# First transfers of the attention: the second stack and one chunk of parts go ahead of the first maxima, two chunks go behind them

## The chip, the cores and the metric

The kernel is one program on one core of a Trainium2 chip. The metric is the time of one execution on the device in microseconds (us), lower is better. The engines are TensorE (PE, with its weight loads PEld), VectorE (DVE), ScalarE (ACT), GpSimd (POOL) and SyncE (SP), which issues nearly all DMA transfers of this kernel.

## What is computed

`x` has 4 sequences of 1024 tokens, 128 wide. The first layer is a causal attention with 16 heads of 8 (the weights go through a rank of 32), between two layer norms and with a residual. The second is two layers of windowed attention and a gated MLP, again between layer norms. The change touches the first layer alone:

```python
x = x + _layernorm(_L0_attn_ref(_layernorm(x), W_dq, W_uq, W_dkv, W_uk, W_uv, W_o))
# in _L0_attn_ref
Q, K, V = (c_q @ W_uq), (c_kv @ W_uk), (c_kv @ W_uv)      # heads of 8
scores = einsum('bqhd,bkhd->bhqk', Q, K) / sqrt(8)         # causal, 1024 x 1024 per head
attn = softmax(scores); out = einsum('bhqk,bkhd->bqhd', attn, V) @ W_o
```

## The kernel before

`project` (L83 to L297) norms the tokens, projects them to Q, K and V, and cuts each f32 value of Q and K into three bf16 parts. It does so in 8 chunks of 512 tokens (two chunks are one sequence). `send_parts` (L72) writes the parts of one chunk to DRAM with six DMAs of 128 KB, three of q (L77) and three of k (L79). The SBUF buffer of parts has 4 places, so chunk 5 is in place 1.

`load_group` (L64) reads them back as a **stack** for one sequence and one group of four heads, with the nine products of parts laid out as 72 rows: one DMA of 576 KB for q (L69, with `q_src` as 24 x 3 x 4096) and one for k (L70, with `k_src` as 3 x 24 x 4096). A stack needs only the chunks of its own sequence, that is chunks 0 and 1 for the first four stacks.

`attend` (L363 to L634) works through 16 stages (4 sequences x 4 head groups) of 12 groups each. For each stage PE makes the scores twice: first `max_unit` (L431, 48 units a stage) into `a_psM`, which DVE reduces to a row maximum (L598, L600), and later `score` (L443) into `a_psE`, which ACT turns into exponentials (L515). The negated maxima reach the second pass as 12 more rows of the q stack. For that POOL cuts them in three, PE turns them (L469), ACT copies them to `a_nmT` (L521), and SP sends them with one DMA of 48 KB into rows 72 to 83 of `a_qs` (`send_maxima`, L398). A stage has two such halves, (s, 0) and (s, 1). `values` (L457) multiplies the exponentials with V two to three groups later.

PE does the first 32 `max_unit`s, turns the maxima (0, 0), and then begins group 0, whose first score waits for `nm_in[0]`, the landing of the maxima (0, 0). The first score of group 4 waits for the maxima (0, 1), that of group 12 for the maxima (1, 0). `max_unit` 48, the first of the second stage, is in group 2 and waits for the second stack.

All this is one hand-written order on SP, and one SP queue carries it. In `project` SP sends chunks 0 to 3, loads the first stack and sends chunk 4. In `attend` it sends chunks 5, 6 and 7, loads the second stack, and then

```python
def send_maxima(s, half):
    sp.wait_ge(e_read, nm_slot(s, half) + 1)      # ACT has copied a_nmT
    ...
    sp.dma_start(qs[ROWS:KROWS, s % NG, :, cols], nmT[...]...).then_inc(nm_in[half], 16)
```

sends the maxima (0, 0) and (0, 1), loads stacks 2 and 3, and waits for the parts of all places (`parts_out`) before the loop over the later stages.

Of the kernel before, what the change touches and what calls it, by code (L numbers as in the profile page):

```python
# [28 lines left out]
NCH = NT // 4  # L29
# [34 lines left out]
def load_group(sp, io, sb, b, g):  # L64

    into = sb["stack_in"][g]
    q_src = io["q_parts"][b, g].rearrange("a d j n -> (a d) (j n)").unsqueeze(1).broadcast_to((3 * DK, 3, HG * S))
    k_src = io["k_parts"][b, g].rearrange("d r j n -> (d r) (j n)").unsqueeze(0).broadcast_to((3, 3 * DK, HG * S))
    sp.dma_start(sb["qs"][0:ROWS, g, :, :], q_src).then_inc(into, 16)  # L69
    sp.dma_start(sb["ks"][0:ROWS, g, :, :], k_src).then_inc(into, 16)  # L70


def send_parts(sp, io, sb, c):

    pair, place, cols, parts_out = c // 2, c % PARTS, slice(512 * (c % 2), 512 * (c % 2) + 512), sb["parts_out"]
    for a in range(3):
        sp.dma_start(io["q_parts"][pair, :, a, :, :, cols].rearrange("g d j n -> g (d j) n"),  # L77
                     sb["parts"][:, place, 0, a, :]).then_inc(parts_out[place], 16)
        sp.dma_start(io["k_parts"][pair, :, :, a, :, cols].rearrange("g d j n -> (g d) j n"),  # L79
                     sb["parts"][:, place, 1, a, :]).then_inc(parts_out[place], 16)  # L80
# [255 lines left out]
def nm_slot(s, half):  # L336

    G = nm_turn_group(s, half)
    before = sum(1 for s2 in range(NSTAGE) for h2 in range(2) if nm_turn_group(s2, h2) < G)
    return (G + 1) * HG + before  # L340
# [19 lines left out]
def attend(nc, io, sb):  # L360


    with ExitStack() as ctx:  # L363
# [29 lines left out]
        @block.sync  # L393
        def _(sp):
            def send_maxima(s, half):
                sp.wait_ge(e_read, nm_slot(s, half) + 1)
                cols = slice(512 * half, 512 * half + 512)
                sp.dma_start(qs[ROWS:KROWS, s % NG, :, cols], nmT[:, s % 2, cols].unsqueeze(1).broadcast_to((NM, HG, 512))).then_inc(nm_in[half], 16)  # L398

            for c in range(5, NCH):  # L400
                send_parts(sp, io, sb, c)
            load_group(sp, io, sb, 0, 1)
            send_maxima(0, 0)
            send_maxima(0, 1)
            for g in range(2, NG):
                load_group(sp, io, sb, 0, g)
            for place in range(PARTS):
                sp.wait_ge(sb["parts_out"][place], 16 * 6 * (NCH // PARTS))
            for e in range(NSTAGE):
                if e + 1 < NSTAGE:  # L410
                    send_maxima(e + 1, 0)
                if e > 0 and e + NG - 1 < NSTAGE:
                    sp.wait_ge(av_done, e * NGR)
                    load_group(sp, io, sb, (e + NG - 1) // NG, (e + NG - 1) % NG)
                if e + 1 < NSTAGE:
                    send_maxima(e + 1, 1)
            for half in range(2):
                sp.wait_ge(nm_in[half], 16 * NSTAGE)
# [1138 lines left out]
```

## Time and profile before

| what | value |
|---|---|
| median of 3 runs | 1483.54 us (1483.34 to 1484.93) |
| the profiled execution, its own time | 1486.43 us |
| its span, first to last instruction | 1484.7 us |
| `project` up to the first matmul of the attention | 0 to 68.7 us |
| the attention's groups, first to last | 100.1 to about 580 us |
| granted TensorE clock, mean | 0.933 of full |

One execution was profiled; all durations below are from it. The span leaves out some 1.7 us around the instructions. A timeline row gives the start, the time, the engine, the line and what is written and read; behind it, in brackets, the idle time before and what ended it. On the SP queue the time of a DMA row is that of its issue, not of the transfer. In a row of merged instructions ("x14") the time is that of all.

### The profile page before, as it was taken

To read this page: it belongs to the slowest core of one execution; us is meant where nothing else is said; L and a number is where in the kernel's file an instruction comes from. 1 tells how busy PE (TensorE), PEld (TensorE's weight loads), DVE (VectorE), ACT (ScalarE), POOL (GpSimd) and SP (SyncE) were. 2 spreads that over 40 slices of the span, in tenths; PEclk is the share of its full clock that TensorE was granted. 3 is DMA by queue.
4 is the path that set the end of the run, shared out by engine and by line. 5 is a ranking of instruction groups with operands and counts; after the bars stand their busy time and mean duration, and the time that the engine had idled before them with its cause. 6 is when DMAs were issued, how large, how long until landed. Compare 5 with 4: busy or idle time off the path is not lost. (4 is left out here: it accounts for less than half of the span.)

```text
span 1484.7 us, 30399 instructions
## 1 busy us (share of the span) xinstructions
PE 1276.6 (86%) x10501; PEld 712.2 (48%) x10501; DVE 1194.1 (80%) x3044; ACT 933.4 (63%) x2597; POOL 744.0 (50%) x742
## 2 busy tenths in 40 slices
PE   4649999999999997469999999699699999997892
PEld 2313333343333333326666666565366666665551
DVE  5758888888888861669999999666599999996667
ACT  4515776777677675647888888332478888883220
POOL 1002212221221221479999999210599999993102
PEclk9858999999999998579999999899899999998996
DMA  4422111112111002001211111000012111110001
GB/s 108 124 80 69 36 57 47 37 36 62 42 37 47 26 5 84 15 22 30 50 30 30 31 30 30 8 1 1 21 27 53 30 30 30 30 30 9 1 1 57
DMA packets 35056, 55.46 MB, mean 37 GB/s; under 512 B 6978, under 2 KB 22732, under 8 KB 32588
## 3 DMA queue, kind: packets, MB, share of 16 engines
q1 hardware_dynamic: 34328, 53.37, 13.6%
q8 instruction: 85, 1.39, 0.4%
q14 instruction: 67, 0.55, 0.1%
q10 hardware_dynamic: 576, 0.15, 0.0%
HBM read 26.77 MB, written 8.39 MB: 24 GB/s over the span
## 5 line engine op out<-in xcount | busy, mean ns | idle before, releaser
L515 ACT ACTIVATE a_prob<-a_psE 128x512 f32<-128x512 f32 (+3 forms) x768 | 318.2, 499 | 151.4 <-PE a_psE L443 148.8
L443 PE MATMUL a_psE<-a_qs,a_ks 84*128 84x512 bf16 (+3 forms) x768 | 247.2, 334 | 31.9 <-DMA a_qs<-a_nmT 18.1
L1085 POOL TENSOR_TENSOR w_t<-w_raw,w_sin 128x256 f32<-128x256 f32 x256 | 240.2, 968 | 46.9 <-ACT w_raw L1011 46.9
L598 DVE CUSTOM_DVE_ANT_0 a_psM<-a_psM,mask_q 128x384 f32<-128x384 f32 (+3 forms) x512 | 242.4, 508 | 19.1 <-PE a_psM L431 18.5
L431 PE MATMUL a_psM<-a_ks,a_qs 72*128 72x512 bf16 (+3 forms) x768 | 249.8, 343 | 5.7 <-PEq L86 3.2
L550 POOL TENSOR_SCALAR_AFFINE_SELECT a_prob<-a_prob 128x512 f32<-128x512 f32 x128 | 81.5, 637 | 329.4 <-ACT a_prob L515 305.0
L600 DVE TENSOR_REDUCE a_nm<-a_psM 128x1 f32<-128x512 f32 x256 | 175.8, 687 | 59.3 <-PE a_psM L431 59.3
L1034 ACT ACTIVATE w_prob<-w_psS,w_bias 128x128 f32<-128x128 f32 x512 | 181.4, 367 | 48.7 <-DVE w_bias L1163 43.2
L1095 POOL TENSOR_TENSOR w_rn<-w_ssm,mhalf 128x16 f32<-128x16 f32 x64 | 189.5, 2962 | 0.0
L443 PEld LDWEIGHTS a_psE<-a_qs,a_ks 84*128 84x128 bf16 x768 | 74.4, 98 | 193.4 <-ACT a_prob L515 97.1
L1090 POOL TENSOR_TENSOR w_rot<-w_t 128x1024 f32<-128x1024 f32 x64 | 152.9, 2389 | 8.8 <-issue 0.4
L457 PE MATMUL a_psO<-a_prob,v_all 128*32 128x512 f32 (+3 forms) x1536 | 145.7, 496 | 0.0
L897 PE MATMUL w_psQK<-w_wqkv,w_hT 128*128 128x512 f32 x256 | 130.3, 632 | 4.2 <-DVE w_hT L1124 3.7
L1147 DVE TENSOR_TENSOR w_rot<-w_rot,w_rn 128x1024 f32<-128x1024 f32 x64 | 101.5, 1586 | 4.4 <-POOL w_rn L1095 2.7
L1034 ACT ACTIVATION_READ_ACCUMULATOR w_prob<-w_psS,w_bias 128x1 f32 x512 | 104.4, 204 | 0.0
L431 PEld LDWEIGHTS a_psM<-a_ks,a_qs 72*128 72x128 bf16 x768 | 76.4, 100 | 56.9 <-DVE a_nm L598 18.5
L1163 DVE TENSOR_REDUCE w_bias<-w_psS 128x4 f32<-128x512 f32 x128 | 87.3, 682 | 7.2 <-PE w_psS L930 7.2
L1138 DVE TENSOR_TENSOR w_t<-w_raw,w_cos 128x1024 f32<-128x1024 f32 x64 | 78.0, 1219 | 16.8 <-ACT w_raw L1011 9.7
L1041 ACT ACTIVATE w_pT<-w_psT 128x512 f32<-128x512 f32 x64 | 38.2, 597 | 78.6 <-PE w_psT L941 78.6
L1271 PE MATMUL f_psU<-f_hT,f_w 128*114 128x512 f32 (+1 forms) x192 | 86.8, 601 | 0.3 <-ACT f_gate L1315 0.3
L909 PEld LDWEIGHTS w_psT<-ident,w_rot 128*128 128x128 f32 x512 | 60.7, 143 | 47.8 <-issue 29.5
L909 PE MATMUL w_psT<-ident,w_rot 128*128 128x128 f32 x512 | 68.4, 278 | 14.5 <-DVE w_rot L1147 14.5
(139 smaller groups left out, 2533.4 us busy)
## 6 DMA issues: line engine op xcount, KB each, us to landing
w_vb<-w_v SPq DMA_DIRECT2D x128, 128.0 KB, 2.3
a_qs<-q_parts SPq DMA_DIRECT2D x16, 576.0 KB
a_ks<-k_parts SPq DMA_DIRECT2D x16, 576.0 KB
q_parts<-p_parts SPq DMA_DIRECT2D x24, 128.0 KB
k_parts<-p_parts SPq DMA_DIRECT2D x24, 128.0 KB
out_x<-l_y SPq DMA_DIRECT2D x8, 256.0 KB, 2.3
a_qs<-a_nmT SPq DMA_DIRECT2D x32, 48.0 KB
w_wqkv<-in_wqkv SPq DMA_DIRECT2D x2, 768.0 KB, 7.5
```

The costliest lines, as they stand in the source:

```text
L431: pe.matmul(out, qs[0:ROWS, g, j, i * P:(i + 1) * P], ks[0:ROWS, g, j, 512 * kc:512 * kc + n], start=True, stop=True).then_inc(m_ready, 1)
L443: pe.matmul(psE[:, r % NRING, 0:w], ks[0:KROWS, g, j, kt * P:(kt + 1) * P], qs[0:KROWS, g, j, q0:q0 + w], start=True, stop=True).then_inc( ...
L457: mm = pe.matmul(psO[32 * j:32 * j + 32, q0:512], v_flat[:, col + j * VA:col + j * VA + 32], prob[G % NPROB][:, j, 0:512 - q0], start=(kt ...
L515: act.activation(prob[G % NPROB][:, j, 0:w], psE[:, r % NRING, 0:w], ACT.Exp, scale=SCALE0).then_inc(e_read, 1)
L598: dve.tensor_tensor_reduce(scores, scores, sb["mask_q"][:, 512 - n:512], -1.0, -3.0 * NEG, ALU.add, ALU.min, low).then_inc(m_read, 1)
L600: dve.tensor_reduce(low, scores, AX.X, ALU.max, negate=True).then_inc(m_read, 1)
L897: pe.matmul(psQK[:, w, :], hT[:, r % 2, 0:P], wqkv[:, bass.ds(layer * (3 * INNER) + w * INNER, INNER)], start=True, stop=True).then_inc(qk ...
L909: i = pe.transpose(psT[:, w, c * P:(c + 1) * P], rot[:, r % 2, w * INNER + c * P:w * INNER + (c + 1) * P], sb["ident"])
L1034: i = act.activation(prob[:, p, w, c, :], psS[:, w, c * P:(c + 1) * P], ACT.Exp, bias=bias[:, p, n:n + 1], accum_out=den[:, p, n:n + 1])
L1085: i = pool.tensor_tensor(out[:, w, :, half, :], src[:, w, :, 1 - half, :], tab, ALU.mult)
L1090: pool.tensor_tensor(rot[:, r % 2, :], t1[:, :], t2[:, :], ALU.add).then_inc(rot_done, 1)
L1095: pool.tensor_tensor(rn[:, r % 2, :], ssm[:, r % 2, :], sb["mhalf"][:, 0:16], ALU.pow).then_inc(rn_done, 1)
```

## The change

```diff
-            for c in range(5, NCH):
+            load_group(sp, io, sb, 0, 1)
+            send_parts(sp, io, sb, 5)
+            send_maxima(0, 0)
+            for c in range(6, NCH):
                 send_parts(sp, io, sb, c)
-            load_group(sp, io, sb, 0, 1)
-            send_maxima(0, 0)
             send_maxima(0, 1)
             for g in range(2, NG):
                 load_group(sp, io, sb, 0, g)
```

No DMA is added or taken away; the same 22 are issued in another order. No other engine's order of instructions changes. On SP, at the start of the attention, before (the last of the 18 part DMAs, then the second stack, the maxima, and the third and fourth stack):

```order
L77 DMA q_parts<-p_parts 4x32x512
L79 DMA k_parts<-p_parts 32x4x512
L69 DMA a_qs<-q_parts 72x1x4096
L70 DMA a_ks<-k_parts 72x1x4096
L398 DMA a_qs<-a_nmT 12x4x512 x2
L69 DMA a_qs<-q_parts 72x1x4096
L70 DMA a_ks<-k_parts 72x1x4096
```

Both maxima transfers stood together, behind all parts and the second stack. The same place now, from the first instruction of the attention's block on:

```order
L393 UNCONDITIONAL_BRANCH
L69 DMA a_qs<-q_parts 72x1x4096
L70 DMA a_ks<-k_parts 72x1x4096
L77 DMA q_parts<-p_parts 4x32x512
L79 DMA k_parts<-p_parts 32x4x512
L77 DMA q_parts<-p_parts 4x32x512
L79 DMA k_parts<-p_parts 32x4x512
L77 DMA q_parts<-p_parts 4x32x512
L79 DMA k_parts<-p_parts 32x4x512
L398 DMA a_qs<-a_nmT 12x4x512
L77 DMA q_parts<-p_parts 4x32x512
L79 DMA k_parts<-p_parts 32x4x512
```

The first maxima have moved ahead of 12 part DMAs (chunks 6 and 7), and the second stack ahead of all 18; the second maxima come behind chunk 7.

## Rows read from the trace of the kernel before

**Rows 1.** Page, part 1: busy time, share of the span, instructions.
```profile
PE 1276.6 (86%) x10501; PEld 712.2 (48%) x10501; DVE 1194.1 (80%) x3044; ACT 933.4 (63%) x2597; POOL 744.0 (50%) x742
```
**Rows 2.** Waits of PE from 84 to 180 us: total, times, longest.
```profile
PE a_psE L443 <- DMA a_qs<-a_nmT: 18.1, 3, 17.5
```
**Rows 3.** Timeline of PE.
```profile
81.98 0.59 PE L469 MATMUL a_psE<-ident_b,a_nmp 128*12 128x128 bf16 x4
...
100.07 0.61 PE L443 MATMUL a_psE<-a_qs,a_ks 84*128 84x512 bf16 x1 [17.50 <-DMA a_qs<-a_nmT]
...
116.51 3.19 PE L457 MATMUL a_psO<-a_prob,v_all 128*32 128x512 f32 x13
119.91 0.39 PE L443 MATMUL a_psE<-a_qs,a_ks 84*128 84x512 bf16 x1 [0.21 <-DMA a_qs<-a_nmT]
...
143.09 0.39 PE L443 MATMUL a_psE<-a_qs,a_ks 84*128 84x512 bf16 x1 [0.42 <-DMA a_qs<-a_nmT]
```
**Rows 4.** Timeline of ACT: the copy of the first maxima.
```profile
82.61 0.59 ACT L521 ACTIVATE a_nmT<-a_psE 12x512 bf16<-12x512 bf16 x1 [16.21 <-PE a_psE L469]
```
**Rows 5.** Timeline of the SP queue, 44 to 86 us: start and length of each issue.
```profile
49.69 1.17 SPq L69 DMA_DIRECT2D a_qs<-q_parts  x1
...
54.60 7.00 SPq L79 DMA_DIRECT2D k_parts<-p_parts  x1
...
62.19 1.19 SPq L79 DMA_DIRECT2D k_parts<-p_parts  x1
68.56 0.51 SPq L77 DMA_DIRECT2D q_parts<-p_parts  x1
...
71.98 2.31 SPq L77 DMA_DIRECT2D q_parts<-p_parts  x1
...
82.16 0.65 SPq L79 DMA_DIRECT2D k_parts<-p_parts  x1
82.86 0.94 SPq L69 DMA_DIRECT2D a_qs<-q_parts  x1
...
85.54 0.88 SPq L398 DMA_DIRECT2D a_qs<-a_nmT  x1
```
**Rows 6.** Timeline of the SP queue, 110 to 230 us.
```profile
117.36 0.80 SPq L398 DMA_DIRECT2D a_qs<-a_nmT  x1
118.20 0.78 SPq L69 DMA_DIRECT2D a_qs<-q_parts  x1
...
157.86 0.78 SPq L69 DMA_DIRECT2D a_qs<-q_parts  x1
```
**Rows 7.** Stretches: length, busy PE, PEld, DVE, ACT, POOL, clock, DMA share, GB/s.
```profile
68.00:69.00 1.00, 0.26 (x3) 0.29 (x4) 0.28 (x1) 0.00 (x0) 0.00 (x0) 0.70 0.11 39
...
86.00:89.00 3.00, 0.00 (x0) 0.00 (x0) 0.00 (x0) 0.00 (x0) 0.00 (x0) 0.50 0.50 166
89.00:92.00 3.00, 0.00 (x0) 0.00 (x0) 0.00 (x0) 0.00 (x0) 0.00 (x0) 0.50 0.20 76
...
99.00:100.00 1.00, 0.00 (x0) 0.00 (x0) 0.00 (x0) 0.00 (x0) 0.00 (x0) 0.50 0.03 12
```
**Rows 8.** Stretches behind the load of the fifth stack, same columns.
```profile
168.00:169.00 1.00, 1.00 (x13) 0.36 (x6) 0.97 (x4) 0.00 (x0) 0.00 (x0) 1.00 0.19 82
169.00:170.00 1.00, 0.86 (x9) 0.31 (x7) 0.96 (x8) 1.00 (x4) 0.65 (x3) 1.00 0.12 49
170.00:171.00 1.00, 1.00 (x11) 0.49 (x14) 1.00 (x7) 0.96 (x5) 0.86 (x2) 1.00 0.00 0
```
**Rows 9.** Stretches by stage of the work, same columns.
```profile
104.70:109.40 4.70, 4.70 (x13) 1.81 (x12) 4.70 (x14) 2.10 (x5) 0.00 (x0) 0.50 0.00 0
...
118.00:120.00 2.00, 1.79 (x13) 0.46 (x6) 0.12 (x2) 0.00 (x0) 1.45 (x5) 0.60 0.43 70
...
120.00:127.00 7.00, 6.64 (x44) 2.42 (x44) 6.45 (x22) 5.05 (x9) 0.00 (x0) 1.00 0.68 160
...
160.00:580.00 420.00, 406.33 (x2956) 158.86 (x2956) 335.61 (x1130) 305.12 (x747) 96.12 (x224) 1.00 0.13 38
```

## The prediction, made before the changed kernel was run

> **What bounds the kernel now.** I read the page's busy times first, then the waits around the place of the change, then the timelines of PE, ACT and the SP queue there, and last the DMA share by stretches. Over the whole span PE and DVE share the load, 86% and 80% busy [rows 1], and neither number says anything about a change at 68 to 120 us. The waits do: PE loses 17.5 us in one piece, waiting for a transfer of `a_nmT`, the first maxima [rows 2]. The timeline shows where: PE has turned the maxima at 82.6 us (81.98 + 0.59) and makes its next matmul, the first score of group 0, at 100.07 [rows 3]. ACT had its copy ready at 82.61 + 0.59 = 83.20 us [rows 4]. DVE and ACT, which live on what PE makes, do nothing meanwhile: both stand at 0.00 in the stretch from 86 to 89 us, and from 99 to 100 [rows 7]. So the kernel stands still for that time, and the transfer alone decides when it goes on.
>
> Why it is late can be read from the SP queue. SP first issues the 18 part DMAs (from 68.56 us), then the second stack (from 82.86), and the maxima only at 85.54 [rows 5]. That is 2.3 us behind ACT's copy. The other 14 us pass after the issue. The same transfer on an empty queue, the maxima (0, 1), was issued at 117.36 and its waiter ran at 119.91, 2.55 us later [rows 6, 3]. After 85.54 the DMA engines are half busy up to 89 us, then at a share of 0.20 with 76 GB/s, and the last packets run between 99 and 100 [rows 7]. A share of 0.20 is some 3 of the core's 16 engines: the tail of the stack runs on few engines, and the maxima share some of them and land when it ends. From the last packet to the first score some 1.0 us pass (99.1 to 100.07).
>
> **The change, part by part.** No DMA is added or dropped. What counts is what lies ahead of the maxima (0, 0) on the queue's slow engines.
>
> 1. The second stack goes from 82.86 to about 68.56, the place of the first part DMA [rows 5]. It is still ahead of the maxima. Its time on the queue: the fifth stack went out alone at 157.86 [rows 6], its last packets run in 169 to 170 at a share of 0.12 after 0.19, so they end near 169.6, and nothing runs from 170 on [rows 8]. That is 11.7 us. The queue is nearly empty when it starts, as the rest of chunk 4 is down to a share of 0.11 at 68 to 69 us [rows 7]. The bound from the other side is the stack of this very place, from 82.86 to about 99.2, 16.3 us, but that one had chunk 7 ahead of it (share 0.50 up to 89 us). I take 11.7, as the queue's state is that of the fifth stack.
>
> 2. Chunk 5 follows it. A chunk behind a stack is seen once: chunk 4, its last issue done at 62.19 + 1.19 = 63.38, last packets near 68.8 [rows 5, 7], so 5.4 us. The three chunks 5, 6 and 7 together went from 68.56, or some 2 us later for the first packet, to about 88: 5.8 us each. I take 5.5. In the first case the fourth part DMA took 7.00 us to issue, at 54.60 [rows 5], because the queue behind the stack was full. The same must happen again: the stack issue took from 49.69 to the end of chunk 4's issue at 63.38, 13.7 us, so SP is free again at 68.56 + 13.7 = 82.3 us at the latest, just ahead of ACT's copy at 83.20. The stall therefore costs nothing; this cover is 0.9 us thick.
>
> 3. SP issues the maxima at about 83.25 in place of 85.54. On an empty queue they would land at 83.25 + 2.55 = 85.8 us, the earliest there can be. The queue gives 68.56 + 11.7 + 5.5 + 1.0 = **86.8 us**. The later one counts. PE starts group 0 at 86.8 in place of 100.07, **13.3 us earlier**. The late bound, with 16.3 for the stack and 5.8 for the chunk, is 91.7 us, 8.4 us earlier.
>
> 4. Chunks 6 and 7 now run beside group 0 and what follows. SP issued them in 71.98 to 82.81, 10.8 us [rows 5], so now from 84.1 to about 94.9; with one more stall of 7 us it is 101.9. The queue is through them at 86 + 11.6, about 98. The maxima (0, 1) are ready 13.3 us earlier than now, near 104.0 (117.36 - 13.3). SP and the queue are free by then in both cases, with 2 us to spare in the worse one. Nobody else waits for chunks 6 and 7: the first stack that reads them belongs to the fourth sequence.
>
> 5. The second stack's own waiter, unit 48 in group 2, is served well before (80 us against some 96). Stacks 2 and 3 are issued right behind the maxima (0, 1) and shift with them. So do the short waits at group 4 (0.21) and group 12 (0.42) [rows 3]: the transfer that ends the latter hangs on stacks 2 and 3, which start from the maxima (0, 1), so both sides of that wait move together.
>
> 6. Does the gain reach the end? From group 0 on nothing waits for a fixed time. PE is 406 of 420 us busy through the rest of the attention [rows 9], the DMA queue is at a share of 0.13, and the later layers begin when the attention ends. All of it moves forward as a block. I give it back nothing.
>
> Sum: -13.3 us. Against the profiled execution's own 1486.43 that is 1473.1, and a span of 1471.4. The median of the runs is 2.9 lower than that execution; against 1483.54 the forecast is **1470.2 us**.
>
> The Trainium skill, DMA: Bandwidth & Descriptors (Why a DMA increments its semaphore by 16 and not by 1), says that a DMA uses the largest number of engines up to 16 that divides the slowest dimension of both sides. By that rule the k half of a stack (3 against 72) runs on 3 engines, and the trace agrees (share 0.19 to 0.20). The specifications there give about 27 GiB/s per engine, and by the rule each of these three moves 192 KB of the k half and 48 KB of the q half: an estimate of 8.5 us for the stack, against 11.7 from the rows. By that figure the queue would be through before the earliest landing, and the gain would be 14.3 us. I stay with the rows.
>
> **The rivals.**
>
> A. *The stack is slower with parts behind it.* For it: the 16.3 us of rows 5 and 7. Against it: the backlog ahead of that one. Landing at 91.7 at worst, so 1475.1 us; between that and the forecast lies everything in which the stall of point 2 also holds SP beyond 83.2.
>
> B. *More than forecast, by the clock.* TensorE's granted clock falls to 0.50 (1.2 GHz) between 68 and 69 us [rows 7], and the groups 0 to 3 run at it though PE is 4.70 of 4.70 us busy from 104.7 on; in 118 to 120 it is 0.60, and 1.00 (2.4 GHz) only after that [rows 9]. If the shorter idle time lets it rise by group 0, those groups gain a little. Not much, as DVE is 4.70 of 4.70 busy there too [rows 9]: at most half of the 3.19 us of `values` before group 4 [rows 3], 1.6 us. With the earliest landing (14.3) the gain is up to 15.9 us: 1467.6. The Trainium skill, TensorE: Matmul & The Clock Gate (Part 1), has the clock rise with sustained activity; the trace has PE busy and the clock at half from 100 to 119 us, so here the rule alone does not carry it.
>
> C. *Slower, by the clock.* The clock rose with or right after the first run of f32 `values` matmuls, 3.19 us from 116.51 [rows 3]. With everything moved by 13.3 us this run may fall so that the clock does not rise. Place: group 4 on. Price: PE is the fuller engine there, 6.64 of 7 us against 6.45 of DVE [rows 9], and at half the clock its matmul time about doubles, so a stretch at 1.2 GHz costs half its own length. The gain is gone when the rise comes more than 27 us later than now relative to the work, and the kernel is slower by over 0.2% from 33 us on. With 40 us it would be 1483.5 - 13.3 + 20 = 1490 us. Against it: `values` come again every second group, some 7 us apart, so five such runs would have to fail.
>
> D. *The change doesn't do what it says:* the maxima (0, 1) are caught behind chunks 6 and 7. For a gain under 3 us they would have to land 10 us after need, with the queue busy to 114 us in place of 98, which is 14 us per chunk against 5.5. That would be 1482.
>
> **How the numbers follow.** Forecast, gain of 12 to 14.5 us: 0.73. A, 8 to 12: 0.13. B, above 14.5: 0.08. D: 0.03. C: 0.03. The range runs from B's 1467.6 to 0.4 above A's 1475.1, for the scatter of the runs (1483.34 to 1484.93): 1467.6 to 1475.5, with C, D and some of A's far side left out. A difference of 0.2% (3 us) is about what a measurement of this kernel can tell from none. Faster: 0.73 + 0.13 + 0.08 = 0.94 and a little of D, 0.95. Same: 0.02. Slower: 0.03.
>
> **What would show it.** In the new trace: the second stack's issue at 68.6; a part DMA of chunk 5 with an issue of some 6 to 7 us, ended by 82.3; the maxima issued at 83.2 to 83.3; the first score at 86 to 88 and PE's idle time before it 3.5 to 5 us in place of 17.50; the waits at groups 4 and 12 still under 1 us; the clock back at 1.00 near 106 us. Wrong would be: a first score after 90 (A), a new wait of PE for `a_nmT` at group 4 (D), or a clock of 0.50 far beyond 110 us (C).

## The result, and the profile after

| | before | changed |
|---|---|---|
| median | 1483.67 us (4 runs, 1483.34 to 1484.93) | 1472.26 us (4 runs, 1470.94 to 1474.24) |
| ratio to before | | 0.9923, 95% interval 0.9905 to 0.9940 |
| the profiled execution, its own time | 1486.43 us | 1473.19 us |
| its span | 1484.7 us | 1471.5 us |

The kernel is faster by 11.4 us, or 0.77%. The prediction was 1470.2 us with a range of 1467.6 to 1475.5. Two further sets of runs of the same kernel gave 0.9919 (0.9902 to 0.9936) and 0.9927 (0.9906 to 0.9948). Over all its 15 runs the mean is 1473.3, against 1483.6 over 72 runs of before on two chips: a gain of 10.3 us, with a standard error of 0.7. One more run of before, in the set r2, took 1690.0 us at a mean granted clock of 0.728 and is left out everywhere. The forecast gain was 13.3. The direction and the place were right; the size was 2 to 3 us too large, and the experiments point to where that comes from.

The line numbers of the attention are one higher after the change. The waits of PE from 66 to 180 us in the changed kernel, total, times and longest:

```profile
PE a_psE L444 <- DMA a_qs<-a_nmT: 4.3, 2, 4.0
```

The 18.1 us of before [rows 2] have become 4.3. The timeline of PE, which answers to [rows 3]:

```profile
66.76 0.58 PE L432 MATMUL a_psM<-a_ks,a_qs 72*128 72x128 bf16 x4 [3.17 <-PEq L86]
...
84.61 0.61 PE L444 MATMUL a_psE<-a_qs,a_ks 84*128 84x512 bf16 x1 [4.03 <-DMA a_qs<-a_nmT]
...
104.50 0.39 PE L444 MATMUL a_psE<-a_qs,a_ks 84*128 84x512 bf16 x1 [0.31 <-DMA a_qs<-a_nmT]
```

In this execution `project` ended 2 us earlier than in the one of before (the attention's first matmul is at 66.76 here), so absolute times can't be compared. The measure used from here on is the **distance**, from the attention's first matmul to the first score of group 0. It is 84.61 - 66.76 = 17.9 us, where the chosen values of the prediction give 86.8 - 68.74 = 18.1. Group 4 follows 19.9 us behind group 0 (104.50 - 84.61) as it did before (119.91 - 100.07 = 19.8), so nothing is given back there, and its wait is 0.31 against 0.21.

The timeline of the SP queue, against [rows 5]:

```profile
66.57 0.80 SPq L69 DMA_DIRECT2D a_qs<-q_parts  x1
...
70.01 6.54 SPq L79 DMA_DIRECT2D k_parts<-p_parts  x1
...
77.15 1.64 SPq L79 DMA_DIRECT2D k_parts<-p_parts  x1
81.23 0.87 SPq L398 DMA_DIRECT2D a_qs<-a_nmT  x1
...
101.91 0.83 SPq L398 DMA_DIRECT2D a_qs<-a_nmT  x1
```

The long issue of the fourth part DMA is there again (6.54 us, before 7.00), and it is as harmless as expected: SP is through with chunk 5 at 78.8, 2.4 us ahead of the maxima. With chunks 6 and 7 it is through at 92.1 (90.50 + 1.61), almost 10 us ahead of the second maxima. From the first maxima's issue to the first score 3.38 us pass (84.61 - 81.23), against 2.55 on an empty queue [rows 3, 6]: chunk 5 ahead of them costs 0.8 us. e4 below, which takes chunk 5 away, agrees.

### The profile page after: what moved, and what is told of

It reads as the page before. It is cut to its first block and busy times, and to the rows that moved or that the text cites. A ratio compares the mean times of both kernels' runs of the same rounds, so it can differ in the third digit from the quotient of the medians.

```text
span 1471.5 us, 30399 instructions
## 1 busy us (share of the span) xinstructions
PE 1280.7 (87%) x10501; PEld 713.2 (48%) x10501; DVE 1193.7 (81%) x3044; ACT 934.1 (63%) x2597; POOL 743.5 (51%) x742
## 3 DMA queue, kind: packets, MB, share of 16 engines
q1 hardware_dynamic: 34328, 53.37, 13.8%
## 5 line engine op out<-in xcount | busy, mean ns | idle before, releaser
L432 PEld LDWEIGHTS a_psM<-a_ks,a_qs 72*128 72x128 bf16 x768 | 76.5, 100 | 57.3 <-DVE a_nm L599 18.5
```

What stands on the lines that cost most here:

```text
L432: pe.matmul(out, qs[0:ROWS, g, j, i * P:(i + 1) * P], ks[0:ROWS, g, j, 512 * kc:512 * kc + n], start=True, stop=True).then_inc(m_ready, 1)
```

## The experiments

Each kernel's time stands beside runs of before on the same chip. e1 to e4 ran on one chip, the rest on another. r1 and r3 are the change again, r2 is the kernel before again, r4 is e4 again.

### The two moves apart

```diff
# e1: the stack alone
+            load_group(sp, io, sb, 0, 1)
             for c in range(5, NCH):
                 send_parts(sp, io, sb, c)
-            load_group(sp, io, sb, 0, 1)
             send_maxima(0, 0)
```

> Order on SP: second stack, chunks 5, 6, 7, then both maxima: the move of the stack alone, with the maxima left behind all parts. Measured as the distance from the attention's first matmul to the first score (31.3 us before, 17.9 with the change). Theory (the maxima land when the bytes ahead of them on the slow engines are through, whatever their kind): stack and three chunks are still ahead, 11.7 + 3 x 5.5 + 1.0 behind the first issue, distance 29.0, so 2 to 3 us better than before, from the packing alone: 1481. Rival (the stack at the tail, on few engines, was the whole delay, and parts drain beside it): the distance falls to 20 or less and the time to 1473.

Measured: 1483.54 us, ratio 0.9993 (0.9973 to 1.0013), so no gain. PE (its first matmul of the attention is at 65.35):

```profile
93.64 0.61 PE L444 MATMUL a_psE<-a_qs,a_ks 84*128 84x512 bf16 x1 [14.51 <-DMA a_qs<-a_nmT]
```

The distance is 28.3 us. The theory's 29.0 was near, and the rival with 20 or less fell: parts ahead of the maxima delay them as a stack does. How they do it is another matter. With a part DMA of 6.57 us issue at 68.58 and 18 parts to send, SP itself came to the maxima only at 88.88, 4.8 us before the score. So here the delay is for the most part SP's own time to issue, and only some 2 us (4.8 less the 2.55 of an empty queue) are the transfers ahead. In the kernel before it is the other way round: 14.5 us lie behind the issue (85.54 to 100.07, [rows 3, 5]). A gain of 2 to 3 us in time was expected from e1, and there was none. That was the first sign that 31.3, from a single execution of before, was no good base.

```diff
# e2: the maxima early, the stack late
-            for c in range(5, NCH):
-                send_parts(sp, io, sb, c)
+            send_parts(sp, io, sb, 5)
+            send_parts(sp, io, sb, 6)
+            send_maxima(0, 0)
+            send_parts(sp, io, sb, 7)
             load_group(sp, io, sb, 0, 1)
-            send_maxima(0, 0)
             send_maxima(0, 1)
```

> Order: chunks 5, 6, first maxima, chunk 7, second stack, second maxima: the maxima early, the stack late. Theory: the queue is through with chunks 5 and 6 before the maxima are ready, so the first score comes 2.6 to 3.0 us behind ACT's copy, distance 17.1; but the stack is issued some 20 us behind the attention's start and lands near 32, while unit 48 (group 2) wants it at about 27: PE gets a new wait of 5 us for the stack, and the time is 1474 to 1476. Rival (the stack has slack to spare, its place doesn't matter): no such wait and 1470 to 1471.5, better than the change.

Measured: 1476.68 us, ratio 0.9953 (0.9932 to 0.9973). PE (first matmul of the attention at 66.63):

```profile
83.70 0.61 PE L444 MATMUL a_psE<-a_qs,a_ks 84*128 84x512 bf16 x1 [3.29 <-DMA a_qs<-a_nmT]
...
100.78 0.40 PE L432 MATMUL a_psM<-a_ks,a_qs 72*128 72x128 bf16 x2 [7.30 <-DMA a_ks<-k_parts]
```

The distance is the expected 17.1. The wait for the late stack is there too, at unit 48, 7.30 us where 5 were expected. So the maxima bring the gain, and the stack's move keeps it from being lost to another wait. Neither is the whole change.

### Nothing but the stack ahead

```diff
# e4
             load_group(sp, io, sb, 0, 1)
-            send_parts(sp, io, sb, 5)
             send_maxima(0, 0)
-            for c in range(6, NCH):
+            for c in range(5, NCH):
                 send_parts(sp, io, sb, c)
             send_maxima(0, 1)
```

> Order: second stack, first maxima, chunks 5, 6, 7, second maxima: nothing but the stack ahead. Theory: the stack is through 11.7 us behind its issue, before ACT's copy, so the first score comes at the empty queue's 2.55 us behind the issue, distance 17.1, some 0.8 better than the change; SP then issues 18 parts in 16 us and the queue needs 18 to 19 us for them, which ends at about the time the second maxima are ready (35 behind the attention's start): a wait of 0 to 2 us at group 4 may take the 0.8 back. Time within 1 us of the change, 1471 to 1473. Rival (the change's chunk 5 costs the first maxima nothing): distance 17.9 as in the change, and the wait at group 4 makes it slower.

Measured: 1469.3 us, ratio 0.9900 (0.9855 to 0.9945), 4 runs. PE (first matmul of the attention at 66.65, group 4 at 103.66):

```profile
83.77 0.61 PE L444 MATMUL a_psE<-a_qs,a_ks 84*128 84x512 bf16 x1 [3.28 <-DMA a_qs<-a_nmT]
```

The distance is 17.1, 0.7 to 0.8 better than the change, and group 4 waits 0.26 us: the 18 part DMAs behind the maxima do no harm. It also shows the stack alone: issued at 66.46, its last packets run in 78 to 79 us at a share of 0.12, so it takes 12.1 us, near the 11.7 of the prediction. e2, with the same distance of 17.1 and one wait of 7.30 us more, is 6.7 us longer than this order (means of 1476.6 and 1469.9): a wait of PE at this place comes out in the time nearly whole. The time was 3 us better than the change's, more than the distance explains, so this order and the change were each run again (the change's further runs, 1473.1 and 1473.0 us, stand below).

> The order stack, first maxima, chunks 5, 6, 7, once more, since its 4 runs gave 1469.3 against the change's 1472.3 and 1473.1, where the distance explains only 0.7. Theory (the difference beyond 0.7 is clock luck): median 1470 to 1472.5, distance 17.1. Rival (this order is better by 3): median 1469.5 or less.

Measured: 1470.76 us, ratio 0.9904 (0.9886 to 0.9922), distance 17.1. Over both sets the mean of 10 runs is 1469.9 against the 1473.3 of the change's 15, a difference of 3.4 with a standard error of 0.9. The median is on the side of the clock theory, the mean on the side of "better by 3". Where both ran side by side, it has 1470.8 against the change's 1473.0. 0.8 us of the 3.4 is the distance. The mean granted clock of these 10 runs is 0.936, that of the 15 runs 0.933, and by the scatter of before (0.55 us per 0.001, see the last section) that goes with some 1.8 us more, an estimate. Why the clock differs stays open.

### Another queue

```diff
# e3: the order of before; SP doesn't send the first maxima, ACT does
-            send_maxima(0, 0)
...
             copy_maxima(0, 0)
+            act.wait_ge(e_read, nm_slot(0, 0) + 1)
+            act.dma_start(qs[ROWS:KROWS, 0, :, 0:512], nmT[:, 0, 0:512]...).then_inc(nm_in[0], 16)
```

> The order of before on SP, but the first maxima are sent by ACT on its own queue, right behind its copy; 18 part transfers and the stack are still ahead on SP's queue. Theory (first in, first out within a queue decides): the maxima need not wait for the queue of SP, and the first score comes 3 to 4 us behind ACT's copy, distance 17.5 to 18.5, time 1470 to 1473, equal to the change. Rival (the slow engines' bandwidth decides, whichever queue sends): the maxima share these engines with the stack and land late, distance over 22, time over 1476.

Measured: 1472.43 us, ratio 0.9929 (0.9906 to 0.9952). The timelines of ACT with its queue and of PE (first matmul of the attention at 65.90), and a stretch (length, busy PE, PEld, DVE, ACT, POOL, clock, DMA share, GB/s):

```profile
80.33 1.42 ACTq L530 DMA_DIRECT2D a_qs<-a_nmT  x1
...
86.40 0.61 PE L442 MATMUL a_psE<-a_qs,a_ks 84*128 84x512 bf16 x1 [6.72 <-DMA a_qs<-a_nmT]
```
```profile
89.00:92.00 3.00, 3.00 (x9) 1.21 (x8) 3.00 (x8) 1.56 (x3) 0.00 (x0) 0.50 0.19 79
```

The distance is 20.5, between the theory's 17.5 to 18.5 and the rival's 22. Both have a share in it. The score runs while the stack's tail is still going (share 0.19 up to 92 us), so the order within SP's queue was what held the maxima back. But the transfer takes 6.1 us from its issue (86.40 - 80.33) where an empty queue takes 2.55 [rows 3, 6], which fits a transfer that shares busy engines. The Trainium skill (DMA: Bandwidth & Descriptors, Issuing engines are not separate DMA queues) says that transfers run on the same 16 engines and interleave whichever engine issued them. The trace agrees: the maxima landed ahead of the end of the stack that SP had issued at 79.20, and 3.5 us later than alone.

### The stack on more engines

```diff
# e5 (in the order of before), e6 (in that of the change), e7 (in that of e4)
-    k_src = io["k_parts"][b, g].rearrange(...).unsqueeze(0).broadcast_to((3, 3 * DK, HG * S))
+    k_src = io["k_parts"][b, g].rearrange(...)
-    sp.dma_start(sb["ks"][0:ROWS, g, :, :], k_src).then_inc(into, 16)
+    for t in range(3):
+        sp.dma_start(sb["ks"][3 * DK * t:3 * DK * t + 3 * DK, g, :, :], k_src).then_inc(into, 16)
...
-                    pe.wait_ge(stack_in[g], 32 * (s // NG + 1))
+                    pe.wait_ge(stack_in[g], 64 * (s // NG + 1))
```

> The order of before, but the k half of each stack goes as three DMAs of 24 rows, each with a source and a target of 24 rows, in place of one with a broadcast of 3 x 24. Theory (the k half is slow because it runs on some 3 engines): the stack takes 4 to 5 us behind the parts in place of 11 to 12, the DMA share shows no long stretch at 0.2, the distance falls from 31.3 to 24 to 25, and the time to 1476 to 1478. Rival (the stack's time is set by its bytes or by the reads from DRAM): distance 30 to 32, time as before.

Measured: 1480.4 us, ratio 0.9972 (0.9956 to 0.9988). PE (first matmul of the attention at 66.02), and the same stretches as in [rows 7]:

```profile
94.33 0.61 PE L444 MATMUL a_psE<-a_qs,a_ks 84*128 84x512 bf16 x1 [14.48 <-DMA a_qs<-a_nmT]
```
```profile
86.00:89.00 3.00, 0.00 (x0) 0.00 (x0) 0.00 (x0) 0.00 (x0) 0.00 (x0) 0.50 0.84 192
89.00:92.00 3.00, 0.00 (x0) 0.00 (x0) 0.00 (x0) 0.00 (x0) 0.00 (x0) 0.50 0.48 93
```

The long tail at a share of 0.2 is gone, which confirms that it was the k half on few engines. But the distance of 28.3 us is that of e1, not the expected 24 to 25, and the repeat of before (r2, below) has 28.5: against it the edit brought the maxima nothing. The stack ends some 12 us behind its issue (81.66 to about 93.7) where r2's takes 13.7 (82.60 to about 96.3), and it was issued 15.6 us behind the attention's first matmul against r2's 14.3, which takes back nearly all of that. So the theory fell. The 3 us in time are clear of the scatter and don't come from the distance; what they come from was not tried. At a share of 0.84 the engines moved 192 GB/s, while a share of 0.20 moves 76 to 82. 4.4 times the share gave 2.4 times the rate. What the engines have in common there was not tried.

> The changed order with the k half as three DMAs. Theory: the stack and chunk 5 are through before ACT's copy, so the distance is the empty queue's 17.1, 0.8 under the change's, and the short wait at group 12 goes; 1 to 2 us better than the change. Rival (more issues on SP hold the maxima): SP has 1.5 us more to issue, ahead of the copy by 3 us or more, so the distance would have to exceed 17.9.

> The order stack, first maxima, chunks 5, 6, 7, with the k half as three DMAs. Theory: distance 17.1 as with the whole stack in this order, since the queue is empty in both; what is left to gain is at group 12, where the first maxima of the second stage hang on stacks 2 and 3: under 1 us. Time equal to e4's 1469.3 within 1 us. Rival: faster stacks let later stages run ahead, 3 us or more better.

Measured: e6 1469.74 us, ratio 0.9901 (0.9879 to 0.9923), distance 84.18 - 67.11 = 17.1; e7 1471.33 us, ratio 0.9900 (0.9875 to 0.9925), distance 84.33 - 67.22 = 17.1. Both distances are as expected. e7 has the stack alone on the queue, as e4 has: issued at 67.03, it is through at 75.0, in 8.0 us for e4's 12.1. In e6 no part DMA of chunk 5 takes longer than 1.51 us to issue, against 6.54 in the change, so the long issue hangs on the slow k half. Once the queue is empty when ACT's copy is done, a faster stack has nothing left to give there. With 4 runs each neither stands out from e4.

### Where the missing 3 us are

> The change as it is, once more, beside variants that differ by about a microsecond, for its scatter and for the clock. Theory (the attention's order fixes its timeline, the rest of the scatter is the granted clock): distance from the attention's first matmul to the first score 17.9 again, median 1470.5 to 1473; runs with a higher mean clock are the shorter ones. Rival (the distance itself varies from run to run): it is off by over 0.5.

> The kernel before, with a profile of its own. The change's distance to the first score is 13.5 us shorter, but its runs are 10.7 us shorter in the mean (40 against 9 runs). Theory (the difference is granted clock: in the change more time at 1.2 GHz falls on busy stretches of the attention): the profile again has few such pieces behind group 0 (19 us and at most one piece of 3.4), against 29.6 and 36 us in the two profiles of the change. Rival (luck: the pieces fall anywhere in either kernel): it has 7 us or more of them beyond the first 19. Distance 31.3 in both.

> The change, third profile. Theory: distance 17.8 to 17.9; of time at 1.2 GHz behind group 0 it again has 29 us or more, with a piece at 26 us behind the first score (110.8 in both profiles so far). Rival (luck): less than 25 us, or none of it at this place. Median 1471 to 1474 in both.

Measured: r1 1473.14 us, distance 85.05 - 67.25 = 17.8; r3 1472.99 us, distance 87.11 - 69.09 = 18.0. The change's distance is firm. The kernel before, run again (1483.55 us, ratio to itself 0.9995, 0.9981 to 1.0009), was not what its first profile showed. PE (first matmul of the attention at 68.35), and the stretches:

```profile
96.86 0.61 PE L443 MATMUL a_psE<-a_qs,a_ks 84*128 84x512 bf16 x1 [14.68 <-DMA a_qs<-a_nmT]
```
```profile
86.00:89.00 3.00, 0.00 (x0) 0.00 (x0) 0.00 (x0) 0.00 (x0) 0.00 (x0) 0.50 0.37 146
89.00:92.00 3.00, 0.00 (x0) 0.00 (x0) 0.00 (x0) 0.00 (x0) 0.00 (x0) 0.50 0.19 82
92.00:96.00 4.00, 0.00 (x0) 0.00 (x0) 0.00 (x0) 0.00 (x0) 0.00 (x0) 0.50 0.18 77
96.00:97.00 1.00, 0.14 (x1) 0.13 (x2) 0.00 (x0) 0.00 (x0) 0.00 (x0) 0.50 0.03 8
```

Its distance is 28.5 us, not 31.3, and its wait 14.7, not 17.5. The stack's tail runs at 77 to 82 GB/s and ends at 96, where in the first profile it ran at 76 and less and dragged on up to 100 at a share of 0.03 [rows 7]. Between the two rows shown there, the first profile has:

```profile
92.00:97.00 5.00, 0.00 (x0) 0.00 (x0) 0.00 (x0) 0.00 (x0) 0.00 (x0) 0.50 0.18 66
```

The two other kernels with the maxima behind everything, e1 and e5, have 28.3. One of these four profiles had the slow tail, and it was the one that the prediction was read from. Of the kernel before itself there are only two profiles; how often it has the slow tail is not known.

The theory of these three expectations, that the clock takes back part of the gain in the change, fell. From group 0 to the last score the profiles of before have 19.5 and 35.6 us at 1.2 GHz, those of the change 29.6, 36.1 and 29.6. So the pieces fall in either kernel, and the mean clock over all runs is no lower in the change (0.933 against 0.931).

### The clock in the first groups

```diff
# e8: e4, and
             turn_maxima(0, 0)
+            for _ in range(7):
+                pe.matmul(psO[:, :], sb["ident_b"], sb["mask_q"], start=True, stop=True)
```

> The same order with seven added bf16 matmuls of 512 columns by 128 rows, into a bank that is overwritten later, in PE's wait for the first maxima; the result isn't changed. Theory (the clock stays at 1.2 GHz through groups 0 to 3 because of what PE did before, and these groups are bound by DVE anyway): distance 17.1 to 17.4, and if the clock rises by group 0, the first score of group 4 comes 1 to 2 us earlier after that of group 0 than the 19.9 us of before. Rival (the half clock holds these groups back): over 3 us earlier. If the clock doesn't rise: nothing.

Measured: 1471.43 us, ratio 0.9915 (0.9901 to 0.9930). PE, and stretches with the clock in the third column from the end:

```profile
82.64 0.39 PE L444 MATMUL a_psE<-a_qs,a_ks 84*128 84x512 bf16 x1 [0.73 <-DMA a_qs<-a_nmT]
...
101.80 0.39 PE L444 MATMUL a_psE<-a_qs,a_ks 84*128 84x512 bf16 x1 [0.26 <-DMA a_qs<-a_nmT]
```
```profile
79.00:82.64 3.64, 2.58 (x11) 0.93 (x9) 1.25 (x5) 0.59 (x1) 0.00 (x0) 0.70 0.12 18
82.64:88.00 5.36, 4.78 (x18) 1.43 (x19) 4.72 (x13) 3.37 (x6) 0.00 (x0) 1.00 0.52 135
88.00:101.80 13.80, 12.79 (x51) 3.76 (x50) 11.93 (x45) 4.21 (x11) 4.13 (x12) 0.51 0.44 125
```

The added matmuls lifted the clock to 2.4 GHz before group 0. Groups 0 to 3 took 19.2 us (101.80 - 82.64) against 19.9, so 5.4 us at the full clock were worth 0.7. Then it fell again, near 88 us, after PE had been 4.78 of 5.36 us busy. The gain is under the theory's 1 to 2 us and far under the rival's 3. The eighth score came 6.75 us behind the first, against 8.18 in e4, so the full clock gave 1.4 us there and half of it was lost again by group 4. So these groups are not bound by TensorE's clock alone. The other 13.8 us ran at 1.2 GHz again, so for them it was not tried. The time is no better than e4's.

## Why the prediction was right or wrong

- **Place and mechanism: right.** The stall of 17.50 us was the first maxima on SP's queue; it is now 4.03. e1 and e2 separate the moves, and both were needed. e3 takes the maxima off that queue, leaves everything else in place, and has a distance of 20.5.
- **Parts 1 to 3, stack and chunk 5: right within 1 us.** In the change they were through in time for a distance of 17.9; the sum gave 18.1. e4 has the stack at 12.1 us for 11.7.
- **Part 2, the stall of SP behind the stack: right.** 6.54 us, cover 2.4 us and not 0.9. Its reason, a full queue, was argued; e6 shows only that the stall goes when the stack is faster.
- **Part 3, the sum: the term that was mis-sized is its other end.** "PE starts group 0 at 86.8 in place of 100.07" took 100.07 as typical. It held a tail some 2.8 us longer than the 28.5 us of the repeat. With 28.5 - 17.9 = 10.6 us the sum meets the measured 10.3 and 11.4. The prediction had the warning in its hands: it noted that this execution was 2.9 us above the median of the runs, and then took the whole 13.3 off that median. The term was 31.3 us as a distance; the repeat has 28.5. That the long tail is the cause of those 2.9 us is not shown, as the clock scatters the runs by as much. Against the profile's own 1486.43 the forecast was 1473.1, and the profiled execution of the change took 1473.19, but that meeting is luck: between the two profiles `project` is 2.0 us shorter, the distance 13.5 shorter, and the rest behind the first score 2.3 longer (1386.9 against 1384.6). Nor does the distance account for every order to the microsecond. With 28.5 for before, e2, e3 and e5 are some 3 to 4 us faster in the mean than their distances and waits give (1476.6, 1472.8 and 1479.7). So that the tail is what the forecast had too much is the likeliest reading, not a proof.
- **Part 4, chunks 6 and 7: right.** Group 4 waits 0.31 us, and at group 12 PE has no wait for the maxima in the change (0.42 before). **Part 6, nothing given back behind group 0:** within the scatter of 2 to 3 us this can't be told.
- **Part 5, the stack's slack: right for the change,** and e2 shows the price where it is gone, 7.30 us.
- **The estimate from the figures of the Trainium skill** (DMA: Bandwidth & Descriptors, Specifications), 8.5 us for the stack and a gain of 14.3, was further off than the rows: the stack alone took 12.1 us in e4. That few engines carry the k half is shown by e5 and e7.
- **Rivals.** A did not come: no landing later than forecast. B's clock did not rise by itself by group 0, and e8 shows 0.7 us for a part of it. C and D did not come. The range had its late side for A. It was not A that took the time from 1470.2 to 1472.3, so that the range held this miss is luck in part.

## What to carry to other kernels

When a small transfer releases an engine, count what is queued ahead of it on the DMA engines that it uses, not on the sequencer alone, and put in front only what another wait needs sooner. Moving one block forward pushes another back, so look for the next reader of each (e2's 7.30 us). When one execution is profiled and lies above the median, part of the stall may be its excess. Profile the kernel before twice: with the 28.5 us of its second profile this forecast would have come within 1 us of the result.

## What was not expected of the hardware

- The same transfers in the same order took 2.8 us longer in the first profile of before than in the second, in a tail at 76 GB/s and less in place of 77 to 82.
- A load spread over 4.4 times the share of the DMA engines (0.84 against 0.19) gave 2.4 times the rate (192 against about 80 GB/s). The share alone doesn't set the rate: in r2 the engines moved 267 GB/s at 0.78, from 85 to 86 us.
- Per 0.001 of mean granted clock a run of before is some 0.55 us shorter (68 runs with a clock on record, 0.925 to 0.940, correlation -0.70). This is about half of the variance of runs from 1477.5 to 1492.4 us. It is a correlation, and which of the two drives the other was not tried.
- In e8 the clock rose while seven matmuls with 128 rows ran. It fell near 88 us after PE had been 4.78 of 5.36 us busy with matmuls of 72 and 84 rows, and stayed at 1.2 GHz while PE was 12.79 of 13.80 us busy with them. How busy a row of the profile calls PE does not tell its clock.
- Still open: why e4's two profiles have 24 and 20 us at 1.2 GHz from group 0 to the last score and the change's three 30 to 36. It may be luck, or where the groups fall. e8 has 13.7 us of it and is no faster than e4 (mean 1472.0 over 6 runs), so this time alone doesn't set the order of the kernels.
